# A decoder layer on one core without the five warm-up matmuls at its start

## What is computed

```python
x = layernorm(x + attn(x, Wq, Wk, Wv, Wo))        # 16 heads of 64, rotary, causal softmax
x = layernorm(x + softmax(x @ ctx.T) @ ctx)       # ctx: 8 sequences of 375 tokens
x = layernorm(x + x @ weight.T + bias + lora(x))  # low-rank adapters of rank 16
```

## Time and profile before

| | us |
|---|---|
| median of 3 executions | 564.5 (564.27 to 565.64) |
| the profiled execution, its own time | 564.91 |
| its span, first to last instruction | 562.7 |
| TensorE busy in the span | 554.3 (99%) |
| mean granted clock of TensorE | 0.999 |

### The profile page before, as it was taken

The page is one execution under the profiler, slowest core; times in us unless marked ns, Lnnn a source line. Parts: engine busy times, 40 slices in busy tenths (PEclk is TensorE's granted clock), DMA queues, the critical chain, the costliest instruction groups (busy, mean ns, idle before and its releaser), DMA issues.

```text
span 562.7 us, 8030 instructions
## 1 busy us (share of the span) xinstructions
PE 554.3 (99%) x3110; PEld 466.6 (83%) x3110; DVE 201.2 (36%) x479; ACT 221.9 (39%) x537; POOL 208.6 (37%) x172
## 2 busy tenths in 40 slices
PE   8999999999999999999999999999999999999995
PEld 5998898988988898988888888768777687877784
DVE  5715224052241421513621543326344514332321
ACT  4335335244253342524645344144563452522221
POOL 0156134252331443311045655153884772600100
PEclk9999999999999999999999999999999999999999
DMA  8612121021110211400009946669757654460001
GB/s 317 219 37 77 38 76 37 1 76 38 63 50 1 75 38 40 149 0 1 1 29 303 217 122 186 166 208 285 198 175 229 173 155 122 168 185 38 0 38 75
DMA packets 23540, 62.00 MB, mean 110 GB/s; under 512 B 3352, under 2 KB 5272, under 8 KB 23504
## 3 DMA queue, kind: packets, MB, share of 16 engines
q1 hardware_dynamic: 23216, 61.23, 35.8%
q10 hardware_dynamic: 288, 0.26, 0.1%
HBM read 54.14 MB, written 3.67 MB: 103 GB/s over the span
## 4 chain that ended last, share of the span: by engine, by line
PE 91%; POOL 5%; DMA 2%; ACT 1%; DVE 1%; issue 0%; SPq 0%; POOLq 0%; ACTq 0%; DVEq 0%
PE bank L429 37%; PE bank L602 23%; PE bank L695 6%; PE bank L529 5%; PE bank L670 5%; PE bank L450 3%; PE bank L480 3%; PE bank L469 2%; POOL cf_lo L1507 2%; POOL ffn L1530 2%; DMA cf_raw<-ctx_feat 1%; PE bank L442 1%; PE bank L647 1%; DMA x_raw<-x_feat 1%; PE bank L715 1%; PE bank L658 1%
## 5 line engine op out<-in xcount | busy, mean ns | idle before, releaser
L429 PE MATMUL bank<-x_hi,w_hi 128*128 128x448 f32 x336 | 126.8, 377 | 0.0
L429 PE MATMUL bank<-x_lo,w_hi 128*128 128x448 f32 x336 | 122.8, 366 | 0.0
L429 PE MATMUL bank<-x_hi,w_lo 128*128 128x448 f32 x336 | 122.5, 364 | 0.0
L602 PE MATMUL bank<-ffn,act_hi 128*128 128x512 f32 x224 | 71.0, 398 | 0.0
L602 PE MATMUL bank<-wo,act_hi 128*128 128x512 f32 x224 | 69.7, 393 | 0.0
L1507 POOL TENSOR_TENSOR cf_lo<-cf_raw,cf_hi 128x752 fp32r<-128x752 f32 x32 | 56.9, 1804 | 33.7 <-ACT cf_hi L951 33.7
L429 PEld LDWEIGHTS bank<-x_hi,w_hi 128*128 128x128 f32 x336 | 63.1, 188 | 7.0
L429 PEld LDWEIGHTS bank<-x_hi,w_lo 128*128 128x128 f32 x336 | 63.2, 188 | 5.0
L429 PEld LDWEIGHTS bank<-x_lo,w_hi 128*128 128x128 f32 x336 | 63.2, 188 | 4.2
L1477 POOL TENSOR_TENSOR w_lo<-w_mix,w_hi 128x1024 fp32r<-128x1024 f32 x14 | 35.9, 2568 | 81.2 <-ACT w_hi L817 81.2
L836 ACT ACTIVATE prob<-prob,shift 112x112 f32<-112x112 f32 x128 | 47.9, 376 | 42.5 <-DVE shift L1234 42.5
(11 more groups left out here) (117 smaller groups left out, 903.0 us busy)
## 6 DMA issues: line engine op xcount, KB each, us to landing
cf_raw<-ctx_feat SPq DMA_DIRECT2D x32, 376.0 KB, 5.2
w_raw<-qkv_w SPq DMA_DIRECT2D x21, 512.0 KB, 3.3
ctx_tok<-ctx_tok SPq DMA_DIRECT2D x24, 448.0 KB
half_raw<-ffn_w SPq DMA_DIRECT2D x16, 256.0 KB, 4.5
x_raw<-x_feat SPq DMA_DIRECT2D x8, 448.0 KB, 6.6
out<-y_t SPq DMA_DIRECT2D x6, 512.0 KB, 3.0
wo_raw<-wo_w SPq DMA_DIRECT2D x8, 256.0 KB, 5.7
half_raw<-wo_w SPq DMA_DIRECT2D x8, 256.0 KB, 5.2
```

The costliest lines, as they stand in the source:

```text
L429: last = pe.matmul(to[:, 0:HT], a[:, k, :], b[:, k, HT * h:HT * h + HT], start=(k == 0 and b is x_hi and a is w_hi[w]), stop=(k == KT - 1 ...
L602: last = pe.matmul(to[:, :], a[:, k, cols], weight(of, n, k, w), start=(k == 0 and a is act_hi and w == 0), stop=(ends and k == KT - 1 and ...
```

## The change

The tile `warm`, its semaphore `warm_set`, VectorE's fill of it and the five matmuls are taken out. TensorE's first matmul is now the first of `first_part`. Nothing else is edited: no transfer, no order, no buffer's place.

```diff
-WARM_UP = 5
...
-        warm = at("warm", [P, HT], F0 + 12288)
...
-        const_in, warm_set = sem("const_in"), sem("warm_set")
+        const_in = sem("const_in")
...
-            pe.wait_ge(warm_set, 1)
-            for _ in range(WARM_UP):
-                pe.matmul(bank[7][:, 0:HT], warm[:, 0:P], warm[:, :], start=True, stop=True)
...
-            dve.memset(warm[:, :], 1.0).then_inc(warm_set, 1)
```

## The result

The changed kernel takes 566.74 us in the median (565.97 to 567.11, 7 executions), against 564.36 us for the kernel before (563.98 to 565.64, 7). The ratio is 1.0037, with a 95% interval of 1.0025 to 1.0048. It is slower by 2.4 us, where 1.5 us was forecast; 566.74 us lies in the range of 565.0 to 567.4 us. The profiled execution took 566.95 us, with a span of 564.7 us, 2.0 us longer than that of before.

What follows compares the result with a forecast made beforehand. The prediction took TensorE to bound the kernel from its first real work to its last matmul. Fill 0, the matmuls' own time 0 and clock +1.5 us, on the median of 564.5 us, gave 566.0 us, range 565.0 to 567.4 us.

Steps and rivals of the forecast that it cites:

- The fill at nothing: VectorE's fill at the start: removing its 0.43 us gains nothing, hidden by the transfer of the first weights.
- The five matmuls' own time at nothing: TensorE's start: without them the first data matmul starts at most 0.13 us earlier, which gains nothing.
- The cover: TensorE's wait for `x_lo` until 8.18 us, 0.39 us idle, hides the first two data matmuls even at the low level.
- The clock: TensorE's first data matmuls: without warm-ups they run at the low clock level, costing 1.5 us, range 1.2 to 1.9 us.
- The share lost: First-stage matmuls: part of each us at the low level that is lost, 0.46 or 0.50.
- the time at the low level: After the first matmul on `x_lo` at 8.18 us: 2.69 or 3.73 us until the clock rises.
- the late rise: Rival at the start: clock rises as late as 15.64 us, costing above 1.9 and up to 3.7 us; chance 0.25.
- the early rise: Rival at the start: clock rises between 8.2 and 10.9 us, costing 0 to 1.2 us; chance 0.19.
- the forecast: Likeliest case: low clock level over the first data costs 1.2 to 1.9 us, time 566.0 us; chance 0.46.
- the change has no effect: Rival: the clock is already up in timed executions, or an unseen pause takes up the delay; 564.5 us, chance 0.08.
- it is faster: Rival: TensorE's early work slows the first transfers, so removal gains at most some tenths of a us; chance 0.02.
- The signs of being wrong: Slow matmuls under 5 or over 11, delay smaller at 556 than 37 us, or start's transfer or ScalarE's rounding moving.

Runs made afterwards that it cites:

- changed, again: The changed kernel, unedited, measured a second time: 566.46 us, ratio 1.0027 to the kernel before; its profiled execution took 566.78 us.
- changed, third: The changed kernel, unedited, run once more for a third profile: 566.15 us.
- fill only: The kernel before with its fill of the tile and TensorE's wait for it, but none of the five matmuls: 566.36 us, ratio 1.0025.
- one, late: The kernel before with one warm-up matmul in place of five, placed behind the wait for the first weights, right before the data: 565.19 us, ratio 1.0010.
- four small matmuls: The changed kernel with four extra matmuls of 64 rows and 112 columns between the first stage's third and fourth slices: 566.85 us, ratio 1.0039.
- four small, again: The changed kernel with the same four extra small matmuls between the third and fourth slices, run once more: 566.43 us.

## Why the prediction was right, and where its sizes were off

**The bound.** TensorE bounds the kernel to its last matmul: right. Of a delay of 2.38 us that had built up by 45 us, all was still there at 420 us. There and behind it 0.40 us of it went, which is the first profile's pause and may not be the change's. With eight warm-ups a delay of 1.4 us was carried in the same way. In all 14 profiles the execution ends 8.88 to 8.94 us after the start of the last matmul, while their times go from 564.22 to 567.53 us.

**The fill at nothing.** Right within what was measured. With the fill kept the ratio is 1.0025, without it 1.0037 and 1.0027.

**The five matmuls' own time at nothing.** Right in the profiled executions. The cover held, though the first two matmuls on data start 0.51 us apart, where at most 0.41 us was forecast. The third still had to wait for `x_lo` (its weight load after the change):

```profile
7.91 0.29 PEld L523 LDWEIGHTS bank<-x_lo,w_hi 128*128 128x128 f32 x1 [0.56 <-DVE x_lo L1159]
```

One thing has to be added: the five hide as long as the clock rises early under them. The more of them run at the low level, the longer they take, and eight show that this reaches the data.

**The clock.** The mechanism was right: without warm-ups the low level lies over the data. The transfers at the start are not what slows the first matmuls: the kernel before runs them 0.203 us apart from 8.49 us on, while as much arrives between 8 and 12 us (400 GB/s, 404 after the change). The share lost was the lower of its two bounds: in the changed kernel's profile these matmuls are 0.373 us apart at half clock, so 0.46 is lost per us. The term that was mis-sized is the time at the low level. I put it at 2.7 to 3.7 us behind the first matmul on `x_lo`, from one warm-up that took 3.7 us to the rise. In the changed kernel's first profile it was 4.5 us (7.91 to 12.45 us), with 12 slow matmuls, above the 11 that I had named as the limit; in its other two profiles there were 11 and 7. It is not a constant. These are all the profiles in which the rise came over data, with the net price as in the table above (the time from the first matmul on `x_lo` to the first step at full pace, less 0.31 + 0.203 x (steps - 1)):

| execution | first matmul on `x_lo` | rise | us between | net price, measured | 0.457 x us between |
|---|---|---|---|---|---|
| changed | 7.91 | 12.45 | 4.54 | 2.06 | 2.07 |
| changed, again | 7.93 | 12.13 | 4.20 | 1.90 | 1.92 |
| changed, third | 7.94 | 10.69 | 2.75 | 1.24 | 1.26 |
| fill only | 8.04 | 13.31 | 5.27 | 2.39 | 2.41 |
| one warm-up | 7.94 | 10.71 | 2.77 | 1.25 | 1.27 |
| one, late | 7.69 | 10.90 | 3.21 | 1.45 | 1.47 |
| four small matmuls | 8.01 | 10.35 | 2.34 | 1.06 | 1.07 |
| four small, again | 7.65 | 10.95 | 3.30 | 1.49 | 1.51 |

The last two columns come from the same starts. That they agree within 0.03 us shows that the starts keep to two paces, not that the time follows; for that stands the pair of profiles above, 0.63 us in the times for 0.66 us by the rise. The time at the low level varied from 2.3 to 5.3 us. What I treated as the late rise (chance 0.25), the early rise (0.19) and the forecast are one mechanism drawn differently in each execution: by price, the three profiles of the changed kernel are one late rise (2.06 us), one at the border to it (1.90 us) and one at the border to the early rise (1.24 us). The Trainium skill says this in TensorE: Matmul & The Clock Gate, Part 1: The HAM clock gate (the count of slow matmuls varies from run to run), and the runs bear it out with 12, 11 and 7 of one kernel. I had cited it, and still sized the term by the one value in the trace.

**The pace.** Missed altogether, some 0.6 us in all three profiles of the changed kernel. Between the two profiled executions 1.5 us was forecast and 1.98 us was measured at the last matmul: 2.06 - 1.5 = 0.56 us is the clock, 0.58 us the pace, and the first transfer and the pause take 0.67 us off again. So it is luck that the last matmul came at 558.01 us, so close to the 557.9 us forecast. The medians of the first comparison differ by 2.4 us because its profiled execution of before was 0.55 us above its median and that of after 0.21 us (2.04 + 0.55 - 0.21 = 2.38). In the third profile the pace adds 0.61 us (the delay grows from 1.00 us at 10.7 us to 1.61 us at the second transposes, 43.98 against 42.37 us). With its terms the times close too: 564.91 + 1.24 + 0.61 - 0.24 (transfer) - 0.40 (pause) = 566.12 us, against 566.15 us measured.

**The rivals.** That the change has no effect, and that it is faster, are excluded by the interval. The early rise, put between 8.2 and 10.9 us, was seen once in the changed kernel: the third profile's 10.69 us, at a price of 1.24 us where at most 1.2 us was given.

**The signs of being wrong.** Three of those that the prediction named came up. The slow matmuls numbered 12. The delay was smaller at the last matmul (1.98 us) than behind the first stage (39.16 - 36.86 = 2.30 us), by the pause at 420 us. The first transfer landed 0.27 us earlier. The last of these comes up between two executions of the kernel before as well, so as a sign it was set too fine. The first is a true miss, of the size and not of the mechanism.

**The size against the 0.3%.** The first comparison gives 1.0037 (1.0025 to 1.0048), the second 1.0027 (1.0016 to 1.0039). The two straddle the bound, as the chances of 0.58 and 0.40 had it.

## What to carry to other kernels

The clock at the start of a program is read from the distance between the starts of equal matmuls, and not from the granted clock, which reads 1.00 there. In this kernel, where TensorE is the bound from its first data on, one warm-up 3.7 us ahead of the data was worth nothing, and one right before it was worth 1.3 us. Four and five cost nothing, since they end before the first data or hardly after it, and eight held up the data. One profile gives one draw of when the clock rises. The term should be sized over the spread, here 1.1 to 2.4 us. A wide spread of the times of a kernel (564.12 to 567.17 us with three warm-ups) is a hint of it without any profile.

## What the runs showed of the hardware that was not expected

**The moment of the rise.** From TensorE's first work to the rise it took 3.7 and 3.5 us in the two profiles of the kernel before, 3.5 and 5.6 us in the two with eight warm-ups, 5.6, 5.2 and 3.8 us in the three of the changed kernel, and from 3.4 us (four small matmuls, first) to 6.3 us (fill only) in all those without warm-ups. So it differs by some 2 us between executions of one kernel.

**Two paces at full clock.** The same stream of 448-column fp32r matmuls runs at 0.203 us or at 0.207 us per matmul, for as long as the stream lasts. The slower one was seen in all five profiles of the changed kernel and of its version with the four small matmuls, and in two of nine profiles that keep the fill (four warm-ups, and the second with eight). The transposes at 39 us did not end it. The scores at 45 us ended it, and so did the four matmuls of 64 rows at 20 us, in two of two profiles. That it ends there is shown. What starts it is open: a rise under data does not by itself (0.203 us in three such executions with the fill kept), and whether five of five against two of nine is chance was not settled. The chip is a rival that no run tests. The four profiles of one chip (fill only, and one, three and eight warm-ups) all have 0.203 us, and the changed kernel was not profiled again there. On the two other chips 0.207 us is in all four without the fill and in two of four with it. Of the first profiles of before (0.203 us) and after (0.207 us) the chip is not on record.
